# The router's struck-out logits move from SBUF to the free half of the gate's PSUM bank

## What is computed

```
logits = einsum('bsd,ed->bse', x, gate_w) + gate_b          # x here: (16, 224, 512)
probs = softmax(logits, axis=-2)                            # over the 224 tokens
vals_t, idx_t = top_k(probs.transpose(0, 2, 1), 8)          # 8 tokens for each of 32 experts
...
merged = einsum('bked,bke->bed', tok, vals)                 # weighted sum of the 8 tokens
h = gelu(concat([merged, ones]) @ w1)                       # expert by expert
o = concat([h, ones]) @ w2
out = scatter_add(out, idx, o * vals)
```

## Time and profile before

| | |
|---|---|
| median of 3 runs | 2262.58 us (2260.3 to 2263.67) |
| profiled execution | 2257.76 us, span of its instructions 2256.1 us |
| TensorE matmuls, busy | 1858.3 us, 82% of the span |
| VectorE, busy | 1028.3 us, 46% |
| ScalarE, busy | 745.9 us, 33% |
| GpSimd, busy | 823.6 us, 37% |
| one loop turn (one batch) | 90.00 us |
| walk over experts | from about 1577 us to the end |

### The profile page before, as it was taken

The page is one execution under the profiler, slowest core; times in us unless marked ns, Lnnn a source line. Parts: engine busy times, 40 slices in busy tenths (PEclk is TensorE's granted clock), DMA queues, the critical chain, the costliest instruction groups (busy, mean ns, idle before and its releaser), DMA issues. The chain is left out here.

```text
span 2256.1 us, 41492 instructions
## 1 busy us (share of the span) xinstructions
PE 1858.3 (82%) x12594; PEld 1211.7 (54%) x12594; DVE 1028.3 (46%) x2541; ACT 745.9 (33%) x1551; POOL 823.6 (37%) x591
## 2 busy tenths in 40 slices
PE   7889999999999999999999999976756656556544
PEld 5667777677677776777777777753211111111111
DVE  1355766667667666666676666642100000000003
ACT  3144444445445444454454543532100000000000
POOL 0255555545555555465555555543000000000000
PEclk9799999999999999999999999977878787787776
DMA  5324333333243243332432433364899999999996
GB/s 172 88 67 109 78 77 95 82 87 95 74 106 77 76 97 81 89 96 74 103 78 76 99 80 82 80 223 146 367 418 421 421 420 423 422 420 421 422 377 252
DMA packets 143265, 421.34 MB, mean 187 GB/s; under 512 B 33036, under 2 KB 79084, under 8 KB 118652
## 3 DMA queue, kind: packets, MB, share of 16 engines
q1 hardware_dynamic: 135580, 411.70, 53.4%
q10 hardware_dynamic: 6656, 8.15, 1.0%
q0 software_dynamic: 992, 1.02, 0.1%
HBM read 307.37 MB, written 17.14 MB: 144 GB/s over the span
## 5 line engine op out<-in xcount | busy, mean ns | idle before, releaser
L1139 DVE TENSOR_REDUCE maxes<-bank 112x1 f32<-112x376 f32 (+1 forms) x1024 | 511.1, 537 | 129.6 <-PE bank L1345 127.0
L943 ACT ACTIVATE probs<-bank 125x448 f32<-125x448 f32 x768 | 399.5, 546 | 156.9 <-PE bank L1367 150.0
L1367 PE MATMUL bank<-q_st,k_st 98*125 98x224 f32 x1536 | 338.6, 307 | 23.5 <-DMA q_st<-max_lo 21.9
L821 POOL TENSOR_TENSOR psum_keys<-psum_keys,probs 125x896 f32<-125x896 f32 x127 | 266.6, 2099 | 214.9 <-ACT probs L943 209.8
L1345 PE MATMUL bank<-k_st,q_st 96*112 96x376 f32 (+1 forms) x1024 | 319.6, 358 | 21.5 <-DVE maxes L1139 18.9
L1753 PE MATMUL bank<-ring,hid_T 128*32 128x512 f32 x1024 | 175.5, 848 | 194.2 <-DMA ring<-in_L_ffn_w 191.0
L1367 PEld LDWEIGHTS bank<-q_st,k_st 98*125 98x125 f32 x1536 | 258.3, 192 | 82.2 <-issue 48.1
L1671 DVE TENSOR_TENSOR o_fin<-bank,b_row 16x512 f32<-16x512 f32 x32 | 21.7, 679 | 586.0 <-PE bank L1711 586.0
L824 POOL TENSOR_TENSOR psum_keys<-psum_keys,probs 125x896 f32<-125x896 f32 x127 | 266.7, 2100 | 9.9
L1593 POOL DMA_DIRECT2D o_rows<-o_fin x31 | 15.2, 492 | 597.7 <-DVE o_fin L1671 597.7
L1345 PEld LDWEIGHTS bank<-k_st,q_st 96*112 96x112 f32 x1024 | 170.2, 181 | 77.9 <-DVE maxes L1139 50.3
(11 more groups left out here) (168 smaller groups left out, 2762.4 us busy)
## 6 DMA issues: line engine op xcount, KB each, us to landing
ring<-in_L_ffn_w SPq DMA_DIRECT2D x128, 2048.0 KB, 30.4
k_st<-k_hi SPq DMA_DIRECT2D x512, 93.8 KB, 2.1
k_st<-k_lo SPq DMA_DIRECT2D x256, 93.8 KB, 2.2
q_st<-q_hi SPq DMA_DIRECT2D x504, 28.0 KB, 1.8
ctx_nat<-in_ctx SPq DMA_DIRECT2D x16, 750.0 KB
x_in<-in_x SPq DMA_DIRECT2D x16, 448.0 KB, 3.7
out<-x SPq DMA_DIRECT2D x16, 448.0 KB, 3.1
out<-ring ACTq DMA_DIRECT2D x28, 256.0 KB, 3.0
```

The lines of the kernel that those rows point to most:

```text
L821: nc.gpsimd.tensor_tensor(psum_keys[:], psum_keys[:], lo, ALU.add).then_inc(pool_chain, 1)
L943: nc.scalar.activation(probs[n % 2][:, j, :], bank[5 + u % 2][0:SK, 0:2 * T], ACT.Exp, scale=SCALE).then_inc(probs_ready, 1)
L1139: nc.vector.tensor_reduce(maxes[:, j, t, c:c + 1], score_bank(n)[0:TT, 0:SC[c + 1] - SC[c]], AX.X, ALU.max).then_inc(s_drained, 1)
L1367: last = nc.tensor.matmul(bank[5 + u % 2][0:SK, kk * T:(kk + 1) * T], k_st[slot][:, j, k * SK:(k + 1) * SK], q_st[slot][:, j, :], start=Tr ...
```

## The change

`beaten` becomes a function of the kind of turn. It gives 32 partitions of the gate's own PSUM bank, columns 224 to 447, beside the logits in columns 0 to 223, which ScalarE has already read when VectorE writes there. L1124 (the next line numbers are four higher behind it: L1128 and L1135) writes to it and L1131 reads it. The bank's next matmuls are those of `wt0` or `wt1`, which wait for the scaled weights; the new assertion says that `wt0` is at most two jobs behind `gate`. Nothing else changes: the instructions of every engine stand in the same order and wait for the same semaphores.

```
+    assert all(q.index("wt0") - q.index("gate") <= 2 for q in (SEQ["mid"], SEQ["last"], SEQ["tail"]))
...
         z_mix = sb(lay, "z_mix", [P, T])
-        beaten = z_mix[0:E, :]
...
-                def router_top(b):
+                def beaten(kind):
+
+                    return bank_of("gate", kind)[0:E, T:2 * T]
+
+                def router_top(kind, b):
...
-                    nc.vector.match_replace(beaten[:], top8[:], logits[:], NEG
+                    nc.vector.match_replace(beaten(kind), top8[:], logits[:], NEG
                                             ).then_inc(router_chain, 1)
...
-                def router_weight(b):
+                def router_weight(kind, b):
...
-                    nc.vector.scalar_tensor_tensor(out=weight[0:E, :], in0=beaten[:], scalar=NEG,
+                    nc.vector.scalar_tensor_tensor(out=weight[0:E, :], in0=beaten(kind), scalar=NEG,
                                                    in1=expo[:], op0=ALU.is_equal, op1=ALU.mult
                                                    ).then_inc(router_chain, 1)
```

More of the change, by code:

```diff
@@ L1197, in step @@
                             if job == "gate":
-                                router_top(b - 1)
-                                router_weight(b - 1)
+                                router_top(kind, b - 1)
+                                router_weight(kind, b - 1)
                         return
```

## The result

The changed kernel took 2241.77 us (median of 4 runs, 2236.67 to 2243.12) against 2262.26 us, ratio 0.9906 with a 95% interval of 0.9889 to 0.9923. That is 20.5 us faster; the forecast was 15.1 us, 2247.5, and its range ended at 2243.0. All 15 runs of the changed kernel have a median of 2241.8 us, and the 30 runs of the kernel before that stood beside them 2260.4. The difference, 18.6 us (16.4 to 20.4 when these runs are drawn again at random), is the better figure.

A forecast was written before the change was run, and what follows sets the result against it. TensorE was taken to bound the batch loop, with 3.17 us idle per 90.00 us batch. 14 x 0.97 = 13.6 plus 1.48 gives 15.1 us, so 2262.58 becomes 2247.5 us, range 2243 to 2255.

The forecast's parts named there:

- The product waits for GpSimd because both its sources are in SBUF: VectorE's masking product L1131: 1.54 of its 1.90 us are waiting for GpSimd's sum; one PSUM source ends that.
- (a): Masking product L1131 with one PSUM source: stops waiting, takes about 390 ns, at most 33 ns above its uncontended 358.
- (b): Striking-out L1124 writing to PSUM instead of SBUF: 8 to 19 ns more than 364 ns, covered by four score maxima.
- (c, d): TensorE's gaps before both router transposes go, 0.69 + 0.28 us; GpSimd moves up some 0.6 us, then catches up.
- 0.97 us a turn: Each of 14 loop turns gains TensorE's two idle gaps at the router's weights, 13.6 us in all.
- (e): Last turn's router: its one gap before the transposes goes entirely, 1.48 us; the sixteenth router, in the tail, gains nothing.
- Partly taken back: Rival: only the first gap goes, or GpSimd's 0.6 us limits the batch; 9.6 to 10.9 us gained, chance 0.17.
- nothing: Rival: masking product L1131 still waits, or the gap opens at the maxima's waits; 2262 us, chance 0.07.
- slower: Rival: striking-out L1124 is much longer with PSUM output; at 2 us the kernel loses 9 us, 2272; chance 0.04.

The follow-up runs named there:

- The stall behind the product: Changed kernel plus an unread VectorE product of the logits, all in SBUF, behind the masking product in loop and last turns: 2253.78 us, ratio 0.9972.
- the other places of the maxima: Changed kernel with group 1's score maxima spread otherwise over its steps: 2239.52 us, ratio 0.9908, a turn 88.60 us.

## Why the forecast was too low

- *The product waits for GpSimd because both its sources are in SBUF*: right. Moving one of them (either), or moving GpSimd's sum out of the way, brings it to 376 to 380 ns. The Trainium skill's rule on who interferes with whom (SBUF — State Buffer) agrees with this: 1896 ns with two SBUF sources beside a sum, 379 with one.
- *A PSUM source costs at most 33 ns* (a): it costs nothing that shows, 379 ns against 380 with both in SBUF (GpSimd waiting), and 358 in both at rest. The 65 ns that I estimated from the Trainium skill (VectorE: DVE Perf Modes, section on the TRN2 errata) did not appear. *The striking-out* (b): 8 ns more, forecast 8 to 19.
- *Both gaps go, and nothing later takes the time back* (c, d): right. GpSimd's second pair of sums started 4.57 us behind the first pair (356.93 against 352.36) instead of 4.95, so it moved up by 0.4 us and not 0.6, but it caught up in its idle time as told, and the other waits kept their length.
- *0.97 us a turn*: this term failed. The turn fell by 1.14 us. I had added up idle times and held the matmuls' 86.83 busy us for fixed, so that only the 3.17 us of idle time could be won. But an idle time is counted from the end of the matmul before, and without a wait the next matmul starts before that end: in the timeline above L1323 starts at 354.50, while L1349 runs to 354.66. From the start of L1283 to the scores' matmul behind the transposes (its line in the kernel before stands below) it was 354.25 - 350.35 = 3.90 us and is 354.94 - 352.20 = 2.74 us now: 1.16. That is 0.17 us too little for each of the twelve turns in the table, 2.0 us. For the first turn the 0.97 were too much: it gained between nothing and 0.5 us, and why is open.

```profile
354.25 0.46 PE L1367 MATMUL bank<-q_st,k_st 98*125 98x224 f32 x2
```

- *1.48 us in the last turn* (e): this term was too small in the pair compared. From the last turn's product to the tail's the time fell by 3.0 us (48.12 to 45.09), and by 3.5 with the last turn alone changed (44.57). The term left out what the clock does: behind the gap the matmuls ran at the lower level (L1384 1.72 us against 0.96), 1.16 us more up to the scores behind the next wait; where the remainder arose is not shown. But with the stall kept there the stretch was 46.51, only 1.4 above the changed kernel, with the same gap and a lower clock as well. So the price of this gap lies between 1.4 and 3.5 us, and no experiment separates the clock's part.
- Corrected, the sum is 12 x 1.14 = 13.7, 0 to 0.5 for the first turn, some 1.1 (an estimate from the other turns) for the one up to the last turn's router, whose length varies by several us from one execution to the next, and 1.4 to 3.5 for the last: 16 to 19 us, against 18.6 in all 15 and 30 runs. The first comparison's 20.5 holds some 2 us of spread. The range's lower end of 2243.0 was too tight for both: for the two terms, and for a kernel whose executions lie up to 13 us apart. (Also, 13 to 17 us gained is 2245.6 to 2249.6, not the 2244 to 2250 given as the forecast's own range.)
- *Partly taken back, nothing, slower*: none came. The stall behind the product shows the first of them in real size: 0.68 us a turn through q_lo alone.

What stays open: why TensorE waits 2 us for the maxima's transfer in one execution and 8 in another of the same program, and whether anything in a kernel favours the one. Also, three kernels with the gap and nine without show that the lower clock goes with it in that place, not how the one brings the other; in the loop, gaps of 0.56 to 0.89 us left the clock at 1.00.

## What to carry to other kernels

Look at minimum against median duration of a line with one shape: a factor of five on VectorE, beside a busy GpSimd, with both sources in SBUF, can be a wait inside the instruction, which the table of waits shows only at the engines behind it. One source in PSUM removed it here, and so did letting GpSimd start later. To price a gap on TensorE, compare start to start with a place where no gap stands: the idle time alone understated it for the change (0.97 against 1.14 us a turn) and overstated it for the other places of the maxima (0.71 against 0.26). Where the granted clock is not steady, the matmuls behind a gap can cost as well.

## What I had not expected of the hardware

The lower clock behind a single gap of 0.53 to 1.48 us in the last turn (granted 0.50 to 0.61 in the 3 us that begin 3 us behind the product), while the loop's gaps of up to 0.89 us, with 96% of the turn busy, and one of 1.65 us later in the last turn left it at 1.00. And GpSimd's next sum is recorded from 352.67, before the stalled product ends at 352.84: as far as the records go, GpSimd did not wait for the product.
